# A recommender tower on one core: VectorE turns the gathered waves in squares of 32, small transfers put them in place, and ScalarE makes part of the one-hot slots

## What is computed

```python
e = jnp.stack([tbl_f[ids[:, f]] for f in range(40)], axis=1)     # (2048, 40, 32)
iidx, jidx = jnp.triu_indices(40, k=1)
z = jnp.einsum('bpd,pde,bpe->bp', e[:, iidx, :], bilinear_matrices, e[:, jidx, :])
h = jnp.concatenate([z, dense_ctx], axis=1)
h = jnp.maximum(h @ W_top1 + b_top1, 0.0)
h = jnp.maximum(h @ W_top2 + b_top2, 0.0)
y = h @ W_top3
```

## Time and profile before

| | |
|---|---|
| median of 3 runs | 1245.42 us |
| lowest, highest | 1243.78, 1253.85 us |
| the profiled execution | 1242.61 us |
| its span, first to last instruction | 1240.8 us |
| mean granted clock of TensorE | 0.814 of full speed |
| gathers on GpSimd (L543) | 496 |
| VectorE: pair products of 1024 elements (L866, L852) | 384 |
| VectorE: one-hot instructions (L835) | 164 |

### The profile page before, as it was taken

One profiled execution on the slowest core, in us unless ns is written; L12 is line 12 of the kernel. 1 busy time (PEld: TensorE's weight loads), 2 busy tenths in 40 slices (PEclk: granted clock), 3 DMA queues, 4 the chain that ended last, 5 costly groups with the idle time before them and its releaser, 6 DMA issues.

```text
span 1240.8 us, 31357 instructions
## 1 busy us (share of the span) xinstructions
PE 960.8 (77%) x14536; PEld 473.6 (38%) x14536; DVE 549.1 (44%) x602; ACT 173.9 (14%) x432; POOL 475.7 (38%) x510
## 2 busy tenths in 40 slices
PE   4226779877887778787796878887788878888998
PEld 3012334333443234343243443443334423344556
DVE  4004345423654336443264443553335623355783
ACT  3011001011101111021010211012101121012211
POOL 7755342445233452434523434225442264322000
PEclk9557677778887879778887777878888878788999
DMA  4005100010000100001000010000100000000000
GB/s 143 14 13 180 34 10 6 10 35 10 6 8 8 35 10 6 9 9 35 11 6 8 8 34 10 6 7 14 32 10 6 6 13 10 8 7 6 4 3 2
DMA packets 24035, 24.54 MB, mean 20 GB/s; under 512 B 11173, under 2 KB 21217, under 8 KB 23777
## 3 DMA queue, kind: packets, MB, share of 16 engines
q0 software_dynamic: 15872, 8.16, 4.4%
q1 hardware_dynamic: 7418, 13.87, 3.4%
q10 hardware_dynamic: 616, 0.51, 0.1%
HBM read 22.44 MB, written 0.06 MB: 18 GB/s over the span
## 4 chain that ended last, share of the span: by engine, by line
PE 71%; issue 15%; another core or an unknown queue 10%; ACT 1%; DVE 1%; DMA 1%; POOL 0%; DVEq 0%; ACTq 0%
PE Y L614 23%; PE ZL L634 21%; PE ZL L660 13%; PE H L590 8%; PE H L573 3%; ACT xcols L742 1%; PE Y L669 1%; DVE prod L866 1%; DMA rows<-tbl,idx 0%; POOL rows L543 0%; PE Y L590 0%; PE Y L678 0%; PE ZL L640 0%; DMA idx<-ids 0%
## 5 line engine op out<-in xcount | busy, mean ns | idle before, releaser
L543 POOL DMA_INDIRECT rows<-tbl,idx x496 | 474.3, 956 | 652.5 <-PE H L573 472.3
L866 DVE TENSOR_TENSOR prod<-Y,xcols 128x1024 f32<-128x1024 f32 x352 | 419.3, 1221 | 538.0 <-remote 347.7
L634 PE MATMUL ZL<-prod,sel 128*32 128x256 f32 x3200 | 325.3, 432 | 48.3 <-issue 43.1
L614 PE MATMUL Y<-xcols,mats 32*64 32x256 f32 x6400 | 313.1, 434 | 29.3 <-ACT xcols L742 12.7
L614 PEld LDWEIGHTS Y<-xcols,mats 32*64 32x64 f32 x6400 | 162.6, 148 | 179.8 <-issue 132.0
L634 PEld LDWEIGHTS ZL<-prod,sel 128*32 128x32 f32 x3200 | 120.3, 120 | 194.9 <-issue 158.7
L660 PE MATMUL ZL<-z,w_sb 128*32 128x256 f32 x1568 | 162.8, 421 | 31.6 <-issue 30.0
L590 PE MATMUL H<-one,parts 125*32 125x256 bf16 x1560 | 97.7, 318 | 80.1 <-issue 80.0
L742 ACT ACTIVATE xcols<-H 32x256 f32<-32x256 f32 (+3 forms) x217 | 81.6, 376 | 546.1 <-PE H L573 335.0
L660 PEld LDWEIGHTS ZL<-z,w_sb 128*32 128x32 f32 x1568 | 66.9, 120 | 99.2 <-issue 73.8
L590 PEld LDWEIGHTS H<-one,parts 125*32 125x32 bf16 x1560 | 51.3, 104 | 128.9 <-issue 126.7
(11 more groups left out here) (43 smaller groups left out, 160.3 us busy)
## 6 DMA issues: line engine op xcount, KB each, us to landing
rows<-tbl,idx POOLq DMA_INDIRECT x496
idb<-ids_turned SPq DMA_DIRECT2D x8, 768.0 KB
w_sb<-w SPq DMA_DIRECT2D x1, 1792.0 KB
mats<-m_wide SPq DMA_DIRECT2D x1, 1152.0 KB
mats<-m_wide SPq DMA_DIRECT2D x1, 960.0 KB
mats<-m_wide SPq DMA_DIRECT2D x1, 768.0 KB, 6.3
tab<-tbl SPq DMA_DIRECT2D x6, 112.0 KB
w_sb<-w SPq DMA_DIRECT2D x1, 512.0 KB
```

Of the source, the lines that this page charges most:

```text
L543: pool.indirect_dma_start(out=rows[:, slot, t, D * q:D * (q + 1)], out_offset=None, in_=tables[f], in_offset=bass.IndirectOffsetOnAxis(ap= ...
L614: last = pe.matmul(Y[2 * D * c:2 * D * (c + 1), bank, cols], mats[D * r:D * (r + 1), u * P + 2 * D * c:u * P + 2 * D * (c + 1)], xcols[D * ...
L634: last = pe.matmul(Z[D * q:D * (q + 1), :], sel[:, GF * (SPAN - 1 - o):GF * (SPAN - 1 - o) + 32], prod[:, (2 * s + bank_of(k, q) // 2) % P ...
L866: dve.tensor_tensor(prod[:, half, :, :].rearrange("p b (u c) -> p b u c", c=BLK), Y[:, pair:pair + 2, :].rearrange("p b (u c) -> p b u c", ...
```

## The change

**Turns.** `flipped(n, j)` is true for all gathered waves of blocks 2 to 7, 45 waves. They leave `items()`. In their place `flip` has VectorE transpose the wave in squares of 32 x 32, one instruction of 256 elements from `rows` to one of 4 places of `squares`, and `place_squares` has SyncE move each square strip to its place in `xcols`: 16 transfers of 32 partitions x 64 numbers for each wave. So that a strip is one run of columns, the samples in a block's columns now stand in another order (`by_square`). TensorE's `multiply` and ScalarE's `mix` wait for these transfers (`s_cols`), the gather of eight waves later waits for the flip (`s_flip`). `flip_steps()` plans the step of each flip.

**Lookups.** `ALL_HOT` goes from (0, 4) to (0, 1, 2, 4, 6), so the third looked-up wave replaces a gathered one in blocks 1, 2 and 6.

**One-hot slots.** From block 2 on those of the second looked-up wave are made by ScalarE (`by_scalar`), with two activations over 1024 elements: |id - place|, then max(0, 1 - that). There is one such slot in the steps w with w % 4 of 1 or 2, up to step 14.

The program of the whole has 112 turning matmuls in place of 496, 2076 lookup matmuls in place of 1752, 472 gathers in place of 496, 45 transposes, 80 one-hot instructions of 1024 elements and 90 of 512 in place of 128 and 36, 96 activations for one-hot slots, and 120 fewer copies of columns by ScalarE.

```diff
-ALL_HOT = (0, 4)
+ALL_HOT = (0, 1, 2, 4, 6)
...
+def flipped(n, j):
+
+    return n > 1 or (n == 1 and j >= TURNED_LATE)
...
+def by_scalar(v):
+
+    n, i, _ = hot_place(v)
+    return n > 1 and i == 1
...
+            def place_squares(v):
+                n, j = flips[v]
+                slot = v % FLIP_RING
+                sp.wait_ge(s_flip, v + 1)
+                if n > 1:
+                    sp.wait_ge(s_prod, 2 * (n - 1) * NS)
+                for f in cold(n)[j]:
+                    g, q = divmod(f, GF)
+                    for c in range(QUARTERS):
+                        sp.dma_start(xcols[D * q:D * (q + 1), n % 2, g, BT * D * c:BT * D * (c + 1)],
+                                     squares[D * c:D * (c + 1), slot, q, :, :]).then_inc(s_cols[slot], DMA)
...
-            for n in range(1, NB):
-                if n < NB - 1:
-                    spread_ids(n + 1)
-                load_dense(n)
+            for n in range(NB):
+                for w in range(NS):
+                    for a in range(2, NB):
+                        if max(HOT_AT[:hot_count(a - 1)]) + 1 == n * NS + w:
+                            spread_ids(a)
+                    if n > 0 and w == 1:
+                        load_dense(n)
+                    for v in [v for v, wave in enumerate(flips) if FLIP_AT[wave] == n * NS + w]:
+                        place_squares(v)
...
                 if k >= RING:
-                    pool.wait_ge(s_turned, k - RING + 1)
+                    a = waves[k - RING]
+                    if flipped(*a):
+                        pool.wait_ge(s_flip, flips.index(a) + 1)
+                    else:
+                        pool.wait_ge(s_turned, k - RING + 1)
...
+                seen = flips_of(n, {g for a in range(w) for g in groups(a)})
+                for v in flips_of(n, groups(w)):
+                    if v not in seen:
+                        pe.wait_ge(s_cols[v % FLIP_RING], cols_landed(v))
...
+            def one_hot(v):
+                n, i, t = hot_place(v)
+                if hot_made(v, True) == 0:
+                    act.wait_ge(s_count, len(count) + 1)
+                act.wait_ge(s_used, v - HOT_RING + 1)
+                act.wait_ge(s_idb[n % 2], (n // 2 + 1) * DMA)
+                slot, ids_at = one[:, v % HOT_RING, :, :], idb[0:HP, n % 2, GF * i:GF * (i + 1), :]
+                act.activation(slot, ids_at, ACT.Abs, bias=off[:, t:t + 1]).then_inc(s_far, 1)
+                act.wait_ge(s_far, hot_made(v + 1, True))
+                act.activation(slot, slot, ACT.Relu, bias=1.0, scale=-1.0).then_inc(s_hot_act, 1)
...
+            def flip(v):
+                n, j = flips[v]
+                slot, k = v % FLIP_RING, wave_number(n, j)
+                dve.wait_ge(s_rows[k % RING], landed(n, j))
+                if v >= FLIP_RING:
+                    dve.wait_ge(s_cols[slot], cols_landed(v - FLIP_RING))
+                dve.transpose(squares[:, slot, :, :, :].rearrange("p q t s -> p (q t s)"),
+                              rows[:, k % RING, :, :, :].rearrange("p q t d -> p (q t d)")).then_inc(s_flip, 1)
```

More of the change, by code:

```diff
@@ L157 @@
 RING = 8
+FLIP_RING = 4
 PROD = 4
@@ L186, in items @@
     at = [[] for _ in range(NB * NS)]
-    turns = [(n, j) for n in range(NB) for j in range(len(cold(n))) if ("turn", n, j) not in HEAD]
+    turns = [(n, j) for n in range(NB) for j in range(len(cold(n))) if not flipped(n, j) and ("turn", n, j) not in HEAD]
     hots = [(n, i) for n in range(NB) for i in hot(n) if ("hot", n, i) not in HEAD]
@@ L295, in tensor_work, with flip_steps @@
     return work
+START = 2700
+GATHERED, GATHER = 1500, 125
+PLACED = 900
+def flip_steps():
+    flips, total = [], 0
+    for n in range(NB):
+        for j, fields in enumerate(cold(n)):
+            total += BT * len(fields)
+            gs = {f // GF for f in fields}
+            first = min([need(fields)] + [max(mixed_at(k), 0) for k in MIXED if gs & {UNITS[u][0] for u in SLOTS[k]}])
+            flips.append((n, j, n * NS + first, GATHERED + GATHER * total))
+    at, now, v = {}, START, 0
+    for s in range(NB * NS):
+        for n, j, first, there in flips:
+            if first == s:
+                now = max(now, there + (PLACED if flipped(n, j) else 0))
+        while v < len(flips):
+            n, j, first, there = flips[v]
+            if flipped(n, j):
+                if s < (n - 1) * NS + 1 or (first > s + 1 and (there > now or s in at.values())):
+                    break
+                at[n, j] = s
+            v += 1
+        now += max(tensor_work(s), PRODUCTS)
+    return at
+FLIP_AT = flip_steps()
+def by_scalar(v):
+    n, i, _ = hot_place(v)
+    return n > 1 and i == 1
 def hot_steps():
@@ L327, with hot_made @@
 HOT_AT = hot_steps()
+def hot_made(v, scalar):
+    return sum(by_scalar(u) == scalar for u in range(v))
 def runs(fields):
@@ L802, in _ @@
                             save_mlp(pn - 1, pw // TILE)
+                    for v in [v for v, s in enumerate(HOT_AT) if s == n * NS + w and by_scalar(v)]:
+                        one_hot(v)
             save_z(NB - 1, ZT - 1)
@@ L885, in _ @@
                         rest(*rests[5])
-                    for v in [v for v, s in enumerate(HOT_AT) if s == n * NS + w]:
+                    for v in [v for v, wave in enumerate(flips) if FLIP_AT[wave] == n * NS + w]:
+                        flip(v)
+                    for v in [v for v, s in enumerate(HOT_AT) if s == n * NS + w and not by_scalar(v)]:
                         one_hot(v)
```

83 lines of the change are left out of this document (55 added, 28 removed).

## The result

The changed kernel took 1324.8 us (median of 4 runs, 1323.7 to 1331.9), the kernel before 1249.6 beside it (4 runs): a ratio of 1.0615, 95% interval 1.055 to 1.068. It is slower; the forecast was 1222 and the range ended at 1270. The profiled execution is 1324.9 us with a span of 1323.0, so 82 us more than before's 1242.6, where the sum said 22 less. On a second chip of the same kind the ratio was 1.064 (1.055 to 1.072).

The account below looks back on a forecast made before the run. The bound was taken as TensorE's work plus about ten microseconds per gathered wave. Terms -13 - 22 + 3 - 3 + 9 + 4 = -22 on 1242.6 gave 1220.6, moved to 1222 us; forecast 1205 to 1235, outer range 1186 to 1270.

Parts of the forecast that it names:

- The bound: Whole kernel: TensorE's work, 597 us of steps, plus about ten microseconds for each gathered wave.
- TensorE's work and the third lookups: Turns leaving TensorE give -22 us, a third looked-up wave in blocks 1, 2 and 6 adds +9: together -13.
- Gathers: 55 waves become 52; the 37 let go by transposes stand alone at 10.2 us, 377 for 399 us: -22.
- VectorE, ScalarE: VectorE's transposes 0.40 us each, +3 us; ScalarE's one-hot passes cost nothing, TensorE's wait for its copies mostly goes, -3.
- SyncE's late places: TensorE waits for columns of flips at block 3 step 7 (+5), step 4 (+1), block 7 step 5 (+3).
- Transfers beside gathers: A flip's transfers issued beside a wave of gathers cost 0.1 us a flip, +4 us.
- C: SyncE's transfers starve TensorE as gathers do, in block 7's eight flips: 54 us, 1276 us; chance 0.13.
- D: A flip's sixteen transfers go one after another, 30 us a flip, SyncE is the bound: 1683 us; chance 0.05.
- point of decision: SyncE's queue: the rival of transfers one after another decides from 19 us a flip, the time between two flips.
- my last doubt: Starving may follow semaphores raised by any transfer: a flip's transfers raise them 256 times, a wave's gathers 128.

Follow-up runs that it names:

- turns kept: The changed kernel without VectorE's turns and the small transfers, all waves turned by TensorE: 1217.0 us, 0.986 of before; on another chip 1218.9 us, 0.990.
- paced: Gathers spread evenly over the steps by GpSimd waits; with TensorE turning, third lookups and ScalarE's one-hots: 684.8 and 683.2 us, 0.991 and 0.987 of before.
- thin transfers: The changed kernel with all sixteen transfers a flip, each 4 partitions instead of 32: 816.4 and 817.9 us, 1.181 and 1.182 of before.

## Why the prediction was wrong

**The bound: right.** Leaving out half the gathers gave back 286 us, and where gathers starve nobody the kernel takes 691 us, the 687 of my sum of work.

**TensorE's work and the third lookups: right.** 224 turning matmuls are left of 992, and the kernel with the third lookups alone is 16 us faster than before.

**Gathers: the count right, the price wrong, at little cost.** All stand alone, 472 of them. But a lone wave isn't dearer than one of three: with turns kept the account gives 9.15 us a wave, before 9.3. My 10.9 came from one stretch. From 350 us on that is 24 us less lost than before without transfers, so the gathers' own term would have been somewhat larger than -22.

**VectorE, ScalarE: right.** Transposes 0.435 us for my 0.40; with and without the one-hot passes, 0.990 and 0.986 overlap. The +3 for transposes and the -3 for ScalarE's copies weren't measured alone.

**SyncE's late places: the times mis-sized, the cost about right, in part by luck.** I took 0.42 us an issue from eight loads of tables in the head; it is 0.59 at the median and 0.65 in a flip, and the landing is 12 us behind the flip for my 8.6. All three places that I named waited: block 3 step 8 for 12.5 us, step 6 for 10.2 (the flip of step 4), block 7 step 8 for 2.2 (the flip of step 5). A fourth, that I hadn't named, waited for 8.5: at the end of the steps, with no gathers to slow them, flips come 8 to 12 us apart, SyncE takes 10 to 12 for each, and the queue fell 5 to 7 us behind. I had priced all at 9 us. The two in block 3 stand beside the gathers that their own flips let go, and cover worked for them as I had said: by the recount those waves lost 12.1 and 10.8 us where the others with transfers lost 10.3 in the mean. With the 8.5 and 2.2 of block 7 that is some 13 us in place of 9: luck in part, since block 3 cost less than I had said and block 7 more. The clock had fallen behind these waits: step 8 of block 3 began with 32 matmuls in 2.04 us instead of 1.15. So it had behind the other waves. Its stretch (columns as above):

```profile
645.97:648.00 2.03, 2.03 (x36) 1.10 (x40) 0.00 (x0) 0.00 (x0) 0.00 (x0) 0.50 0.04 8
```

The granted clock is 0.50, 1.2 GHz.

**Transfers beside gathers: the step that failed.** I took +4 from one 768 KB load whose issue held up one gather by 0.13 us. The row spoke of the gather, not of TensorE, which is what starves, and of one issue, not sixteen. By the account the transfers cost 1.4 us a wave beside the gathers, 52 us over 38 waves, some 2 of them the two waits in block 3. Of the 56 to 60 us outside, some 41 are the lower clock behind the starved waves, 11 the waits of block 7, the rest isn't split. Less 20 us of TensorE's work that is a cost of 90 us, 0.12 a transfer, where I had 4 us for what the transfers do beside the gathers. The sum has no term for the clock at all: 9.5 us a wave held what before lost to it, and I didn't ask what deeper starving does to the work behind. That the deeper starving is what keeps the clock low for longer is read from their order in the traces; no run changed the one without the other.

**The rivals.** C named the right cause with the wrong place: it expected the loss where transfers run alone, in block 7, and took the others as covered since TensorE was starved there anyway. Block 7's steps ran at full pace but for two late places; the covered ones cost, though not the 300 us that C held out for them. Starving was not all or nothing: it had room to become deeper. D, that SyncE's rate is the bound, doesn't hold where before takes 1240 us, and does where it takes 691, with 10 to 12 us a flip for D's 30. What I called its point of decision, 19 us between two flips, is a distance that the starving itself had made. The semaphores that transfers raise, my last doubt, stay untested: in every kernel here where TensorE starves they go with the number of transfers.

The rule of the Trainium skill that spoke against the change (*DMA: Bandwidth & Descriptors*, Rules for kernel authors: make many small transfers one) was right in its direction. The 2 us for each of the same page's Anatomy of one DMA (given for transfers issued from GpSimd) don't add up one after another here: sixteen from SyncE take 10.5 us.

What stays open: why a run of gathers starves TensorE of instructions on one kind of chip and not on the other; whether spreading gathers helps where they do; and what in a transfer deepens the starving, its issue, its bytes or its semaphores (thin transfers were seen only on the other kind, where the bytes made no difference to the issue).

**A version better than both.** The kernel before with the third wave looked up in three more blocks and turns left on TensorE: 0.986 (0.980 to 0.993), and 0.987 to 0.991 (paced, with ScalarE's one-hots) where before takes 691 us.

## What to carry to other kernels

Taking work off a starved engine doesn't pay if it comes back as DMA issues: price each issue by a row of its own kind and count all sixteen, for the time until data is there as well as for what they do to the instructions running beside. "It is starved there anyway" is no cover; ask how much of the work still gets through, for that can be lost too, and ask for how long the clock stays down behind it. And check a distance in time (19 us between two flips) for what made it: remove that cause, and the queue behind it may be the bound.

## What the runs showed of the hardware

- The same kernel takes 1230 to 1250 us on three chips and 691 on two; the difference is TensorE's "issue" idle time beside gathers from GpSimd, with gathers of equal length (0.94 us) and spacing on both (on the second kind seen with the kernel before, paced).
- Where it occurs, eight gathers in a row cost TensorE 9 to 11 us and four about 3.
- A transfer of 8 KB within SBUF takes SyncE 0.59 us to issue at the median (0.51 to 1.7 in the changed kernel), 0.65 in a flip of sixteen, 0.68 when flips queue up; with 4 partitions instead of 32 it takes 0.58. A flip's columns were there 11.7 to 12 us behind it.
- Sixteen such transfers beside eight gathers cost 1.4 us more a wave; without gathers TensorE ran at full pace beside them (21.5 matmuls per us over 14.5 us).
- Behind starved waves TensorE's granted clock is at its lower level, and 32 fp32 matmuls take 2.0 us for 1.1. From 350 us on its mean was 0.79 in the changed kernel and 0.86 with turns kept.
